# Residual graph layer with layernorm: the rows of the six main groups are stored in one transfer

## The reference

```
agg = adj @ (x @ W_agg)
y   = x + w * relu(agg) + (1 - w) * x
out = (y - mean(y)) / sqrt(var(y) + 1e-5)      # over the 64 features of a row
```

## Time and profile before

| | us |
|---|---|
| median of 3 runs (645.44 to 645.63) | 645.47 |
| profiled execution, its own time | 645.12 |
| span of that execution, first to last instruction | 643.3 |
| TensorE matmuls busy | 524.6 (82%) |
| VectorE busy | 51.1 (8%) |
| ScalarE busy | 13.3 (2%) |
| moved by the transfers | 272.89 MB, mean 424 GB/s |

### The profile page before, as it was taken

One profiled execution on the slowest core, in us unless ns is written; L12 is line 12 of the kernel. 1 busy time (PEld: TensorE's weight loads), 2 busy tenths in 40 slices (PEclk: granted clock), 3 DMA queues, 4 the chain that ended last, 5 costly groups with the idle time before them and its releaser, 6 DMA issues.

```text
span 643.3 us, 7562 instructions
## 1 busy us (share of the span) xinstructions
PE 524.6 (82%) x3526; PEld 272.4 (42%) x3526; DVE 51.1 (8%) x87; ACT 13.3 (2%) x25; POOL 0.7 (0%) x7
## 2 busy tenths in 40 slices
PE   4999978868779868778886976977976977797977
PEld 3845434434334434334443433433433433343426
DVE  0230000300000300000300000300000210000202
ACT  1100000000000000000000000000000000000000
POOL 0000000000000000000000000000000000000000
PEclk9999989899798988898889989979889888998999
DMA  9999999999999999999999999999999999999995
GB/s 379 421 431 444 416 441 437 418 433 443 430 425 446 415 438 433 446 415 443 435 438 415 443 430 425 446 429 427 430 446 415 443 422 443 420 442 406 428 421 208
DMA packets 11548, 272.89 MB, mean 424 GB/s; under 512 B 1680, under 2 KB 2320, under 8 KB 3728
## 3 DMA queue, kind: packets, MB, share of 16 engines
q1 hardware_dynamic: 10224, 270.57, 97.9%
q10 hardware_dynamic: 1312, 2.13, 0.9%
HBM read 270.60 MB, written 2.10 MB: 424 GB/s over the span
## 4 chain that ended last, share of the span: by engine, by line
DMA 72%; PE 27%; issue 0%; DVE 0%; SPq 0%; ACT 0%; DVEq 0%
DMA ring<-adj_main_dram 65%; PE bank L198 21%; DMA ring<-adj_mid_dram 5%; PE bank L187 2%; DMA xres<-x_dram 1%; PE bank L171 1%; PE bank L244 1%; PE bank L232 0%; PE bank L265 0%; PE bank L254 0%; SPq L132 0%; DVE xw L319 0%; SPq L147 0%; DVE xres L367 0%; ACT std L287 0%
## 5 line engine op out<-in xcount | busy, mean ns | idle before, releaser
L198 PE MATMUL bank<-ring,xw 128*64 128x320 f32 x3072 | 466.0, 466 | 96.4 <-DMA ring<-adj_main_dram 95.3
L198 PEld LDWEIGHTS bank<-ring,xw 128*64 128x64 f32 x3072 | 231.8, 147 | 328.6 <-DMA ring<-adj_main_dram 117.8
L345 DVE TENSOR_TENSOR y<-bank,w_sb 128x320 f32<-128x320 f32 x12 | 5.3, 486 | 534.6 <-PE bank L207 534.6
L232 PE MATMUL bank<-ring,xw 128*64 128x384 f32 x128 | 22.1, 491 | 4.9 <-DMA ring<-adj_mid_dram 4.9
L232 PEld LDWEIGHTS bank<-ring,xw 128*64 128x64 f32 x128 | 8.6, 136 | 17.7 <-issue 8.9
L171 PE MATMUL bank<-ident,xres 128*128 128x128 f32 x32 | 8.6, 431 | 9.1 <-DMA xres<-x_dram 9.1
L187 PE MATMUL bank<-wagg,xT 64*128 64x64 f32 x128 | 15.5, 424 | 0.0
L293 ACT ACTIVATE aggT<-bank 128x640 f32<-128x640 f32 x6 | 4.2, 703 | 536.7 <-PE bank L198 536.7
L187 PEld LDWEIGHTS bank<-wagg,xT 64*128 64x128 f32 x128 | 14.2, 326 | 2.3 <-issue 2.0
L171 PEld LDWEIGHTS bank<-ident,xres 128*128 128x128 f32 x32 | 5.8, 218 | 9.8 <-issue 9.1
L207 PE MATMUL bank<-ident,aggT 128*128 128x128 f32 x30 | 4.6, 283 | 4.4 <-ACT aggT L293 4.4
(11 more groups left out here) (29 smaller groups left out, 19.0 us busy)
## 6 DMA issues: line engine op xcount, KB each, us to landing
ring<-adj_main_dram SPq DMA_DIRECT2D x47, 5120.0 KB, 38.5
ring<-adj_mid_dram SPq DMA_DIRECT2D x8, 1536.0 KB, 33.6
ring<-adj_main_dram SPq DMA_DIRECT2D x4, 1280.0 KB, 34.6
xres<-x_dram SPq DMA_DIRECT2D x1, 2048.0 KB, 8.2
out_dram<-xres ACTq DMA_DIRECT2D x6, 320.0 KB, 16.7
ring<-adj_last_dram SPq DMA_DIRECT2D x1, 1024.0 KB, 27.1
ring<-adj_last_dram SPq DMA_DIRECT2D x1, 832.0 KB, 28.8
ring<-adj_last_dram SPq DMA_DIRECT2D x1, 640.0 KB, 29.9
```

The lines of the kernel that those rows point to most:

```text
L198: last = nc.tensor.matmul(acc[h * D:(h + 1) * D, b, 0:CHUNK], xw[:, j], ring[:, slot, at:at + CHUNK], start=j == 0, stop=j == T - 1)
L232: last = nc.tensor.matmul(mid_acc[h * D:(h + 1) * D, b, 0:MID_CHUNK], xw[:, j], ring[:, c // MID_RUN, at:at + MID_CHUNK], start=j < 2, sto ...
```

## The change

The six stores of main groups on ScalarE's queue are gone: in the loop over the groups ScalarE only takes the square root and still waits for `out_ready`. In their place SyncE issues one store of slots 0 to 59 (1.97 MB, 128 pieces of 15,360 bytes) on its own queue, after the eight mid loads and ahead of the ten last loads. It waits for the sixth group's `out_ready` before that. The stores of the mid and of the last group stay on ScalarE. The last wait counts three stores instead of eight.

```diff
+        out_rows = out.rearrange("(p t) d -> p t d", p=P)
...
                 sp.dma_start(ring[:, c // MID_RUN, at:at + SUB * MID_SLOTS * P],
                              adj_mid[c].rearrange("q s n -> q (s n)")).then_inc(mid_loaded[c], 16)
+            sp.wait_ge(out_ready, G)
+            sp.dma_start(out_rows[:, 0:MID_T0], xres[:, 0:MID_T0]).then_inc(stored, 16)
             sp.wait_ge(slot_free, G * C)
...
-            out_rows = out.rearrange("(p t) d -> p t d", p=P)
-
-            def finish(g, t0, n_slots, var, scale, var_step):
+            def std_of(n_slots, var, scale, var_step):
                 act.wait_ge(dve_step, var_step)
                 nc.scalar.activation(std[:, 0:n_slots], var, ACT.Sqrt, bias=eps[:, 0:1], scale=scale).then_inc(std_ready, 1)
+
+            def store(g, t0, n_slots):
                 act.wait_ge(out_ready, g + 1)
-                act.dma_start(out_rows[:, bass.ds(t0, n_slots)], xres[:, bass.ds(t0, n_slots)]).then_inc(stored, 16)
+                act.dma_start(out_rows[:, t0:t0 + n_slots], xres[:, t0:t0 + n_slots]).then_inc(stored, 16)

             with act.Fori(0, G) as g:
...
-                finish(g, g * MAIN_SLOTS, MAIN_SLOTS, varsum[:], 1.0 / D, g * DVE_GROUP + (DVE_PRE + VAR_STEP))
+                std_of(MAIN_SLOTS, varsum[:], 1.0 / D, g * DVE_GROUP + (DVE_PRE + VAR_STEP))
+
+                act.wait_ge(out_ready, g + 1)
...
-            finish(MID, MID_T0, MID_SLOTS, varsum[:, 0:MID_SLOTS], 1.0 / D, MID * DVE_GROUP + DVE_PRE + VAR_STEP)
+            std_of(MID_SLOTS, varsum[:, 0:MID_SLOTS], 1.0 / D, MID * DVE_GROUP + DVE_PRE + VAR_STEP)
+            store(MID, MID_T0, MID_SLOTS)
...
-            finish(LAST, LAST_T0, 1, mv[:, 1:2], 1.0, LAST_STEP0 + LAST_VAR_STEP)
-            act.wait_ge(stored, 16 * (LAST + 1))
+            std_of(1, mv[:, 1:2], 1.0, LAST_STEP0 + LAST_VAR_STEP)
+            store(LAST, LAST_T0, LAST_SLOTS)
+
+            act.wait_ge(stored, 3 * 16)
```

## The result

The changed kernel takes 647.44 us (median of 10 runs, 646.6 to 649.62) against 645.44 us (median of 10, 645.23 to 645.65): ratio 1.0035, 95% interval 1.0027 to 1.0044. The forecast was 646.7, the range 644.8 to 648.3. The runs of the kernel before lie within 0.4 us; those of the changed one spread over 3 us.

What follows compares the result with a forecast made beforehand. Loads were taken to bound the kernel up to the mid group's end, TensorE the last 9 us. Terms -4.65 + 4.6 + 1.5 - 0.2 = +1.25 us gave a forecast median of 646.7 us, range 644.8 to 648.3.

Steps and rivals of the forecast that it cites:

- The bound: Whole kernel: loads set the pace up to the end of the mid group, TensorE in the last 9 us.
- The stores' leaving: Main and mid groups: six stores off ScalarE's queue let loads come earlier by their bytes' time, -4.65 us.
- The long store: Ahead of the last loads: one 1.966 MB store costs its bytes at the loads' rate, +4.6 us.
- The bounds of 2.3 and of 5.3 to 6.0 us: Long store's limits: half overlapping loads (rival, chance 0.12), or dearer than its bytes (rival, chance 0.20).
- The fixed cost of a transfer: All main-group stores: the skill page's about 2 us each would give 10 us less; the prediction rejected it as throughput cost.
- The new wait: SyncE before the long store: waiting for the sixth group's rows is covered by mid loads in flight, 0 us.
- The start: Last group: TensorE starts with its first load's landing instead of 0.2 us after, -0.2 us.
- The clock: Start of the last group: TensorE's clock falls to 1.2 GHz after the wait, costing +1.5 us.
- the idle time: Between mid and last group: TensorE has no work for 4.3 us, where before there was none.
- low twice as long: Rival in the last group: the clock stays low twice as long, 1.4 us more, 648.0 us; chance 0.08.
- slower: Whole kernel: outcome slower by over 0.2%, beginning at 646.76 us; chance 0.50.

Runs made afterwards that it cites:

- the double store: Changed kernel with its long store followed on the same queue by a second one of the same rows to a scratch tensor; 654.15 us median, ratio 1.0124.

## Why the prediction was right

Each step by its term:

- **The bound** was right: loads up to the end of the mid group, TensorE in the last. The two kernels with nearly the same gap, in the last group and in the mid group, show it.
- **The stores' leaving** was put at -4.65 and measured -4.36. The main groups gave 3.87 (I had 4.01 in the single intervals), the mid group 0.49 instead of 0.75. This is the term that was most mis-sized, +0.29. Behind 615.75 the mid group shrank by 0.79, about as priced; ahead of it, from 583.72 on, the same work took 0.30 more (32.33 us against 32.03), and no run says why. The ten traces of kernels without the six stores and with nothing new ahead of the last mid load have its matmuls at 623.10 to 623.43, so 4.15 to 4.48 us earlier than in the one trace of before.
- **The long store** was put at +4.6 and measured 4.60 (7.03 less the 2.63 of before is 4.40, and the 0.20 of the earlier start is in that). Its own landing agrees: issued at 610.50, it took 17.3 us, so it landed at 627.8, 4.6 us after the last mid load. The bounds of 2.3 and of 5.3 to 6.0 us are both ruled out, with the second store (4.54) as well. So neither the difference of the two small last stores nor the stores' share of the page gives the rate of a long one.
- **The fixed cost of a transfer.** The 2 us of the Trainium skill ("DMA: Bandwidth & Descriptors", "Anatomy of one DMA") are no cost of throughput here: six stores cost 4.5 us against none. The section gives them for transfers that GpSimd issues, and puts most of them down to the wait until the write is confirmed; here ScalarE and SyncE issue. The prediction's estimate of 10 us from it left both out.
- **The new wait** costs nothing. The rows were ready at 610.47, the store was issued at 610.50, and the mid loads went on to 623; the rate has no dip (449 GB/s from 609 to 611). I had put it at 609.1. The difference is TensorE's: its last 128 matmuls of the main groups took 20.41 us instead of 19.14, at a granted clock of 0.85 instead of 0.91.
- **The start** came with the landing (630.2, start 630.25), so the 0.2 us of before are gone, as forecast.
- **The clock** was put at +1.5 and measured +1.69 in the profile, as the rule of the Trainium skill ("TensorE: Matmul & The Clock Gate", "HAM oscillation"), that a stretch behind a wait for loads starts cold, had it too, and the idle time at 4.3, measured 4.24. Filling the gap took all of it back, so it is shown, not only argued.

The sum was +1.25; -4.36 + 4.60 - 0.20 + 1.69 is +1.73, which is the profiled difference. The two errors, 0.29 and 0.19, have the same sign, so the forecast did not come out by their cancelling. The median moved a little further, 2.0 us: the profiled execution was the second fastest of its ten, and the slowest is 2.8 us above it. The case "low twice as long" had 8 chances in 100 at 648.0; in the two series of the changed kernel 5 of 16 runs lie above 648.2, though that these are this case is not shown. I had sized the clock's term by its commonest outcome and gave it no spread upward beyond that case. That "slower" had only 0.50 comes from a forecast 0.06 us under the edge of what can be told from no change.

## What to carry to other kernels

Where transfers were the bound, moving a store among them gained nothing, on either queue, but it moved a hole: ask what the engine that waits does next, and whether it is the bound there. Put transfers that nobody waits for behind the last load, under the compute and the final chain that no load can fill; here this was worth 0.7%. Count each stretch in which the transfers run empty before spending effort on the size or the queue of a store.

## What the runs showed that I had not expected

The clock did not come back soon after the double store: it stayed at 0.50 through 3.68 us of unbroken work of TensorE and, by the mean of 0.66, through some 5.6 of the next 8.29 us (to 644, as its windows show), while in the four profiles of the changed kernel it was back within 3.6 us. Why is open. Nor did it fall after every wait of 3.28 us or more, as it had in the trace of before: in the trace after, two main chunks behind such a wait took 8.83 and 8.84 us. A single trace had made this look more regular than it is.

```profile
276.74 8.83 PE L202 MATMUL bank<-ring,xw 128*64 128x320 f32 x64 [3.30 <-DMA ring<-adj_main_dram]
...
494.99 8.84 PE L202 MATMUL bank<-ring,xw 128*64 128x320 f32 x64 [3.28 <-DMA ring<-adj_main_dram]
```

An added matmul took 0.53 us, twice its namesake of 320 columns in the main groups (0.276 for the two instructions). The added ones all wrote to the same 64 partitions, the main groups' alternate between the two halves; that this is the cause was not tested alone. The granted clock read 1.00 over them.
